# A transformer block on one core: Newton step for the inverse deviation, and set-up work in other places of the program

## The reference

```
x = x + _dwconv(x, pos_w, pos_b)                       # 3 x 3, per channel
x = x + _masa(_layernorm(x, ln1_g, ln1_b), mask_h, mask_w, ...)
y = _layernorm(x, ln2_g, ln2_b)
y = gelu(y @ fc1_w + fc1_b) @ fc2_w + fc2_b            # 64 -> 256 -> 64
return x + y

def _layernorm(x, g, b):
    m = mean(x, -1);  v = mean(square(x - m), -1)
    return (x - m) * rsqrt(v + EPS) * g + b            # EPS = 1e-6
def _masa(x, ...):       # 8 heads of 8 channels
    q, k, v = x @ q_w + q_b, (x @ k_w + k_b) * SCALE, x @ v_w + v_b
    lepe = _dwconv(v, lepe_w, lepe_b)                  # 5 x 5
    attn_w = softmax(q k over each row    + mask_w);  vw  = attn_w v
    attn_h = softmax(q k over each column + mask_h);  out = attn_h vw
    return (out + lepe) @ out_w + out_b
```

## Time and profile before

| | us |
|---|---|
| median of 3 runs (lowest, highest) | 2103.77 (2100.58, 2105.39) |
| profiled execution, its own time | 2106.22 |
| its span in the trace | 2104.4 |
| PE busy / DVE / ACT / POOL | 1852.3 / 1428.2 / 1247.0 / 1173.6 |
| data moved by DMA | 346.82 MB |

### The profile page before, as it was taken

One profiled execution on the slowest core, in us unless ns is written; L12 is line 12 of the kernel. 1 busy time (PEld: TensorE's weight loads), 2 busy tenths in 40 slices (PEclk: granted clock), 3 DMA queues, 4 the chain that ended last, 5 costly groups with the idle time before them and its releaser, 6 DMA issues. The chain is left out here.

```text
span 2104.4 us, 89182 instructions
## 1 busy us (share of the span) xinstructions
PE 1852.3 (88%) x34510; PEld 1548.6 (74%) x34510; DVE 1428.2 (68%) x2270; ACT 1247.0 (59%) x2107; POOL 1173.6 (56%) x1858
## 2 busy tenths in 40 slices
PE   5877624999999999999999999999978995599998
PEld 5877522888887888877887877878768995477776
DVE  3588864777776777766777766767642663688885
ACT  4677734555555555564555555555544766488887
POOL 6477855554555554454555554555534001599997
PEclk8888755999999999999999999999988998799999
DMA  9589566678787787778787787776748994466663
GB/s 141 99 197 223 160 190 148 158 172 180 177 178 167 176 178 177 161 179 186 182 186 175 177 186 172 181 185 161 184 89 148 201 233 142 111 137 137 137 137 82
DMA packets 661152, 346.82 MB, mean 165 GB/s; under 512 B 562462, under 2 KB 613406, under 8 KB 660878
## 3 DMA queue, kind: packets, MB, share of 16 engines
q1 hardware_dynamic: 627782, 298.69, 65.1%
q0 software_dynamic: 31936, 43.83, 7.0%
q10 hardware_dynamic: 1160, 0.13, 0.1%
HBM read 105.42 MB, written 102.76 MB: 99 GB/s over the span
## 5 line engine op out<-in xcount | busy, mean ns | idle before, releaser
L813 ACT ACTIVATE att_prob<-att_st_ps 128x448 f32<-128x448 f32 x896 | 486.9, 544 | 439.0 <-PE att_st_ps L720 438.9
L888 DVE TENSOR_REDUCE att_mm<-att_s_ps 128x8 bf16<-128x448 f32 x896 | 556.2, 621 | 266.9 <-PE att_s_ps L690 263.2
L733 PEld LDWEIGHTS att_pv_ps<-att_vx,att_prob 128*56 128x56 f32 x14336 | 562.0, 132 | 89.2 <-issue 5.6
L733 PE MATMUL att_pv_ps<-att_vx,att_prob 128*56 128x18 f32 x14336 | 514.4, 202 | 5.8 <-ACT att_prob L813 4.3
L582 POOL DMA_DIRECT2D att_mvt<-att_mneg x256 | 136.3, 537 | 555.3 <-ACT att_mneg L802 484.9
L690 PE MATMUL att_s_ps<-att_kx,att_q_unit 120*56 120x448 bf16 x1792 | 347.2, 360 | 9.1 <-DMA att_q_unit<-att_qk_hi 7.4
L715 PE MATMUL att_st_ps<-att_mvt,set_both 122*56 122x448 bf16 x1792 | 345.7, 357 | 9.6 <-DMA att_mvt<-att_mneg 8.3
L720 PE MATMUL att_st_ps<-att_qx,att_k_hi 128*56 128x448 bf16 x1792 | 344.4, 356 | 0.0
L720 PE MATMUL att_st_ps<-att_qx,att_k_lo 128*56 128x448 bf16 x1792 | 342.1, 353 | 0.0
L573 POOL DMA_DIRECT2D att_qx<-att_q_hilo x512 | 245.8, 488 | 2.0 <-issue 1.7
L796 ACT ACTIVATE att_qk_hi<-att_pj,set_bias 128x392 bf16<-128x392 f32 x256 | 150.2, 587 | 124.9 <-PE att_pj L648 124.7
(11 more groups left out here) (209 smaller groups left out, 3196.4 us busy)
## 6 DMA issues: line engine op xcount, KB each, us to landing
att_xt<-xn_chunks SPq DMA_DIRECT2D x128, 196.0 KB, 3.4
att_k_hi<-att_qk_hi SPq DMA_DIRECT2D x128, 196.0 KB, 3.5
att_k_lo<-att_qk_lo SPq DMA_DIRECT2D x128, 196.0 KB, 3.8
att_qx<-att_q_hilo POOLq DMA_DIRECT2D x512, 49.0 KB
pos_x<-in_x_dram SPq DMA_DIRECT2D x128, 105.0 KB
lepe_x<-v_scratch SPq DMA_DIRECT2D x128, 105.0 KB, 4.2
x_scratch<-pos_x SPq DMA_DIRECT2D x128, 98.0 KB
...
```

Source lines behind the costliest of these rows:

```text
L733: ins = pe.matmul(pv_ps[v % 2][64 * h:64 * h + L, at:at + 18], prob[t % 4][:, 4 * h + a, :], vx[v][:, VW * j + 36 * a + 18 * h:VW * j + 36 ...
L813: act.activation(out, src, ACT.Exp).then_inc(exp_done, 1)
L888: dve.tensor_reduce(mm[v % 2][:, NH * j:NH * j + NH], s_ps[j % 2][:, 0:S8].rearrange("p (s k) -> p s k", k=L), AX.X, ALU.max).then_inc(max ...
```

## The change

Four parts.

**Inverse deviation.** POOL's pow is replaced. ACT computes sqrt(v + EPS) (`root`, after the second convolution copy of the image, or behind the high half where the last batch has no copies), DVE takes its reciprocal r0 (`flip`, at the end of DVE's image), and POOL does one Newton step r = r0 (1.5 - 0.5 (v + EPS) r0 r0) in five operations on 128 x 28 (`inverse`). `st` gets a fourth row.

**Masks.** `setup.masks` moves from the identity to behind POOL's sixteen relays of the first batch.

**Start of the attention.** The projections of chunks 2 and 3 on PE (and their high halves on ACT, low halves and values on DVE) go between the first chunk's scores and the second chunk's instead of behind the first maxima; the transposed mask rows are written earlier on DVE; the clear of the second key buffer on ACT is split in two, with the first chunk's negation between; POOL clears its query buffers earlier.

**Feed-forward set-up.** A new class `MlpSetup` holds the parameters' buffers. SP issues their 16 DMAs in the second convolution at n = 7; DVE does the splitting in single steps of that stage at n = 0 and 9 to 14; the identity is shared. In the feed-forward SP starts with four row loads, and its x loads wait only for the memsets of the x buffers.

```diff
+            p = slice(64 * h, 64 * h + 64)
+            sp.dma_start(self.wo_f[p, :], self.wo_d).then_inc(par, 16)
...
+    def settled(self, dve):
+        dve.wait_ge(self.prep, self.steps)
+
+    def clear(self, dve):
+        dve.memset(self.bias_f[:, :, :].rearrange("p n c -> p (n c)"), 0.0).then_inc(self.bias_zero, 1)
+        self.done(dve.memset(self.ones_b[:, :], 1.0))
+        self.done(dve.memset(self.wo2[:, :], 0.0))
...
+    def weights(self, dve, n):
+
+        if n == 0:
+            self.clear(dve)
+        elif n == 9:
+            self.high(dve)
+        elif n == 10:
+            self.low_out(dve)
+        elif n == 11:
+            self.low_first(dve)
...
-                sp.wait_ge(x_clear, 2)
+                sp.wait_ge(x_clear, 3)
                 keys_and_units(i, 1)
...
+                clear(qx[0], q_clear)
                 pool.wait_ge(x_clear, 1)
                 fill_k(pool, i, 0, K_POOL, kx_in_sw)
                 for t in vx:
                     pool.memset(t[:, :], 0.0).then_inc(vx_clear, 1)
-                clear(qx[0], q_clear)
                 pool.wait_ge(q_clear, 1)
                 fill_q(i, 0)
+                clear(qx[1], q_clear)
+                pool.wait_ge(q_clear, 2)
                 pool.wait_ge(mvt_set[0], 1)
                 fill_max(i, 0)
                 pool.wait_ge(ones_set, 1)
                 build_vx(i, 0)
                 build_vx(i, 1)
-                pool.wait_ge(x_clear, 2)
+                pool.wait_ge(x_clear, 3)
                 fill_k(pool, i, 1, K_POOL, kx_in_sw)
                 build_vx(i, 2)
                 pool.wait_ge(vx_done, 12)
-                clear(qx[1], q_clear)
-                pool.wait_ge(q_clear, 2)
                 pool.wait_ge(mvt_set[1], 1)
...
                 for j in range(PAIRS):
                     scores(i, 0, j)
+                    if 2 <= j < 6:
+                        project(i, j // 2 + 1, j % 2)
                 maxima(i, 0)
-                for v in range(2, 4):
-                    for th in range(2):
-                        project(i, v, th)
-                for v in range(2, 4):
-                    project_v(i, v)
                 for j in range(S_EARLY):
                     scores(i, 1, j)
+                    if j in (2, 4):
+                        project_v(i, j // 2 + 1)
...
-                clear(kx[0])
+                clear(kx[0], 0, NH)
                 for v in range(2):
                     for th in range(2):
                         high(i, v, th)
                 unit_rows(q_unit[0])
                 mask_k(0, 0, 4)
-                clear(kx[1])
-                negate(i, 0)
+                clear(kx[1], 0, NH // 2)
                 for v in range(2, 4):
                     for th in range(2):
                         high(i, v, th)
+                negate(i, 0)
+                clear(kx[1], NH // 2, NH)
                 unit_rows(q_unit[1])
...
+                mask_rows_t(0, 0)
                 for v in range(2):
                     for th in range(2):
                         low(i, v, th)
                 for v in range(2):
                     values(i, v)
                 dve.wait_ge(cleared, 8)
+                mask_rows_t(1, 0)
                 for j in range(PAIRS):
                     line_max(i, 0, j)
-                mask_rows_t(0, 0)
+                    if 2 <= j < 6:
+                        low(i, j // 2 + 1, j % 2)
...
-                for v in range(2, 4):
-                    for th in range(2):
-                        low(i, v, th)
-                for v in range(2, 4):
-                    values(i, v)
                 for j in range(S_EARLY):
                     line_max(i, 1, j)
-                mask_rows_t(1, 0)
+                    if j in (2, 4):
+                        values(i, j // 2 + 1)
...
+                    if n == 7:
+                        mlp.parameters(sp)
...
                 identity_on(pool, ident, zeroed, setup.unit)
-                setup.masks(pool)
...
+            def inverse(n):
+
+                u = n % 2
+                var, r, r0 = st[u][:, 1, :], st[u][:, 2, :], st[u][:, 3, :]
+                pool.wait_ge(sd_done, n + 1)
+                pool.tensor_scalar(var, var, EPS, -0.5, ALU.add, ALU.mult).then_inc(eps_done, 1)
+                pool.wait_ge(eps_done, n + 1)
+                pool.wait_ge(flipped, n + 1)
+                pool.tensor_tensor(r, var, r0, ALU.mult).then_inc(newton, 1)
+                pool.wait_ge(newton, 3 * n + 1)
+                pool.tensor_tensor(r, r, r0, ALU.mult).then_inc(newton, 1)
+                pool.wait_ge(newton, 3 * n + 2)
+                pool.tensor_scalar(r, r, 1.5, None, ALU.add).then_inc(newton, 1)
+                pool.wait_ge(newton, 3 * n + 3)
+                pool.tensor_tensor(r, r, r0, ALU.mult).then_inc(rs_done, 1)
...
                 relay(pool, 0, cg, relaid)
             if pos:
+                setup.masks(pool)
                 ahead(0)
...
                         low(pool, n - 1)
-                    pool.wait_ge(var_in, n + 1)
-                    pool.tensor_scalar(st[u][:, 1, :], st[u][:, 1, :], EPS, None, ALU.add).then_inc(eps_done, 1)
-                    pool.wait_ge(eps_done, n + 1)
-                    pool.tensor_tensor(st[u][:, 2, :], st[u][:, 1, :], half[:, :], ALU.pow).then_inc(rs_done, 1)
+                    inverse(n)
                     rezero(n)
                     ahead(n + 1)
...
+            def root(n):
+
+                u = n % 2
+                if n == 0:
+                    act.wait_ge(eps_set, 1)
+                act.wait_ge(var_in, n + 1)
+                if n >= 2:
+                    act.wait_ge(xn_done, n - 1)
+                act.activation(st[u][:, 2, :], st[u][:, 1, :], ACT.Sqrt, bias=eps[:, 0:1]).then_inc(sd_done, 1)
...
                     for cg in range(4):
                         conv_copy(b + 1, 4 * q + cg)
+                        if pos and cg == 1:
+                            root(n)
                         if not pos and q < 2 and cg % 2 == 0:
                             high(n + q + cg // 2)
                 if pos:
+                    if b + 1 == NBATCH:
+                        root(n)
                     ahead(n + 1)
...
+            def flip(n):
+                dve.wait_ge(sd_done, n + 1)
+                if n >= 2:
+                    dve.wait_ge(rs_done, n - 1)
+                dve.reciprocal(st[n % 2][:, 3, :], st[n % 2][:, 2, :]).then_inc(flipped, 1)
...
                         col_copy(n - 2, range(2, G))
+                    flip(n)
...
-            sp.wait_ge(bias_zero, 1)
-            for k in range(3):
-                sp.dma_start(bias_f[32 * k:32 * k + 1, 0, :], bo_d.unsqueeze(0)).then_inc(par, 16)
-            sp.dma_start(b2[:, :], bf2_d.partition_broadcast(128)).then_inc(par, 16)
-            sp.wait_ge(gaps, 1)
-            for v in range(NV - 1):
+            for v in range(4):
+                sp.dma_start(rt[v][:, :], rt_d[v]).then_inc(rt_in[v], 16)
+            sp.wait_ge(cleared, 4)
+            for v in range(4):
+                for r in range(2):
+                    sp.dma_start(x1[v][64 * r:64 * r + L, :, :], x1_v[v, r]).then_inc(x1_in[v], 16)
+            for v in range(4, NV - 1):
                 load(0, v)
...
             for t in x1[0:4]:
-                done(dve.memset(t[32:64, :, :].rearrange("p j c -> p (j c)"), 0.0))
+                dve.memset(t[32:64, :, :].rearrange("p j c -> p (j c)"), 0.0).then_inc(cleared, 1)
             for t in (*o_ps[0:2], *y_ps):
-                done(dve.memset(t[:, :], 0.0))
-            settled()
-            dve.sem_inc(gaps, 1)
-            dve.wait_ge(par, 16 * 16)
...
-            for k in range(3):
-                done(dve.tensor_copy(bias_3[32 * k:32 * k + 32, :, :], bias_p[k][32 * k:32 * k + 32, :, :]))
+                dve.memset(t[:, :], 0.0).then_inc(cleared, 1)
+            dve.wait_ge(cleared, 8)
+            dve.sem_inc(ready, 1)
             dve.wait_ge(pre_pe, 1)
-            done(dve.tensor_tensor(b1[:, :], h_ps[0][:, 0:2], b1_in[:, :], ALU.add))
-            dve.wait_ge(unit, 1)
-            done(dve.tensor_copy(ident_b[:, :], ident[:, :]))
-            settled()
-            dve.sem_inc(ready, 1)
+            dve.tensor_tensor(b1[:, :], h_ps[0][:, 0:2], b1_in[:, :], ALU.add).then_inc(biased, 1)
             front(0, 0)
             front(0, 1)
```

176 lines of the change are left out of this document (98 added, 78 removed).

## The result

The changed kernel took 2079.09 us, the median of 4 runs (2071.65 to 2082.95), against 2103.81 before: a ratio of 0.988, 95% interval 0.9849 to 0.9911. That is 24.7 us less, where 28.8 were forecast. Its profiled execution, the slowest of the four, took 2082.95, with a span of 2081.2 against 2104.4. The span is thus 23.2 us shorter. Where they lie is told by the starts of the stages, SP's first issue in each (DVE's first memset for the feed-forward).

| stage | before | after | difference | forecast |
|---|---|---|---|---|
| positional convolution, layernorm | 318.4 | 297.3 | -21.1 | -19.8 |
| attention | 1247.0 | 1245.0 | -2.0 | 0 |
| second convolution | 221.5 | 230.9 | **+9.4** | +0.2 |
| feed-forward | 317.6 | 308.1 | -9.5 | -10.3 |

The account below looks back on a forecast made before the run. It took a loop between engines through POOL's pow to bound the positional convolution; 17.8 (Newton) + 2.0 (masks) + 0 (attention) + 10.1 (feed-forward set-up) = 29.9 us less, stated as 2075, range 2065 to 2090.

Parts of the forecast that it names:

- the lock moves: Positional convolution: POOL's relays now slow DVE's centring instead of its scale, 1.9 us per image, giving 2080; chance 0.25.
- the set-up does not do what it says: Feed-forward start: x's loads wait for other stores, only 5 of the 10 us come, giving 2080; chance 0.05.
- own mechanism: Whole kernel: the forecast's gains come as described, without the rivals' losses, giving 2067 to 2079; chance 0.47.
- The loop through pow is the bound, and DVE is next: Positional convolution: an engine loop of 12.73 us sets the tail's pace; without pow, DVE's own work of 11.8 does.
- Stretches: Positional convolution, four consecutive windows: gains of 2.3, 5.7, 3.4 and 6.4 us, the second ending in a DMA wait.
- Table loads cost nothing: ACT, convolution and attention's start: separate loads for Sqrt and Exp fall where ACT waits for PE; 0, at worst 2.6.
- Masks: Positional convolution's start: four mask DMAs issued later let the first relay come 2.1 us earlier; gain 2.0 (0 to 2.1).
- Attention: Attention's start: earlier projections only lengthen PE's wait for the DMA of the unit's queries; 0, bounds -3 and +3.
- Feed-forward: Feed-forward's start: sixteen parameter DMAs leave its head, so the first residual sum comes earlier; gain 10.3 (8.5 to 11).
- The second convolution: Second (lepe) convolution: takes on 16 SP issues and some ten DVE operations of the feed-forward set-up; cost 0.2 us.
- The bounds: Whole kernel: the bounds of the parts added in full are given as 17 and 35 us of gain.
- Newton: Positional convolution: root, reciprocal and five POOL operations replace pow, 2.4 us for 5.1 per image; stage gain 17.8.

Follow-up runs that it names:

- e2: Changed kernel with the inverse deviation by pow on POOL as before, all else as changed: positional stage 318.5 us, 18.9 us more than e1 in the medians.
- g1: Changed kernel with both convolutions' tiles aligned by 32-byte buffers, plus DVE's reciprocal moved between an image's last two column copies: ratio 0.9853 to the kernel before.
- e1: Changed kernel once more, unaltered: second convolution 229.8 us, ratio 0.9886 to the kernel before.
- e3: Changed kernel with the feed-forward's parameters issued and split at the head of the feed-forward again: 2094.91 us, second convolution 230.7.

## Why the prediction was right, and where it was not

The prediction gave 2075 (2065 to 2090), the measured time is 2079.09, and its sum of 29.9 us stands against 24.7. The number alone would fit the rivals "the lock moves" and "the set-up does not do what it says" (2080 each) better than the own mechanism (2067 to 2079); only the stages tell them apart. By its steps:

- **The loop through pow is the bound, and DVE is next.** Right: with pow put back the stage is 20.0 us longer (e2), where 17.8 were forecast. The tail's loop is 11.56 for 11.8, and the reciprocal, which was bounded by 0.2 and 0.5 and taken at 0.3, takes 0.32.
- **Stretches.** 3.4, 5.6, 3.9 and 7.1 for 2.3, 5.7, 3.4 and 6.4. The second is best supported: its end was forecast from SP's chain and the DMA share, and the relay there did change its waiting from POOL to DMA.
- **Table loads cost nothing.** Right. The drain of 1.38 us that the Trainium skill ("ScalarE: Activation LUTs", What ACT_TABLE_LOAD costs) gives did not show behind the first either: the root began 0.01 us later. Nor does it lie ahead of a load: the second, at 329.81, began 0.01 us after ACT's operation before it had ended.
- **The lock moves.** Right as a mechanism. As a rival's price it was too dear: with 1.9 us on each image it gave 0.5 and 0 us for the first and third stretches, which gained 3.4 and 3.9, and the excess over both operations grew from 12.6 to 15.6 us only. The rule of the Trainium skill ("SBUF — State Buffer", Who interferes with whom) agrees with the row at 132.70 in that the two shut each other out: the centring took 1.92 us more beside relays of 1.96. That the first to issue wins, which the prediction took from there and saw in the earlier trace rows, these rows do not show: by their recorded starts both the scale and the centring had begun first, by 0.07 and 0.09 us, and it was they that took longer. The row of g1 at 144.68 agrees with it: there the centring was first by 0.25 us and POOL waited.
- **Masks.** The relay's 2.0 was right (2.15), but the forecast let it through to the end. The first mean came 1.2 earlier, because PE's granted clock rose no earlier (37.4 us, 37.6 before) and the earlier convolutions ran on the lower level for longer; the forecast had no term for that.
- **Attention.** 0 was right; the bounds of 3 held. That PE would wait longer was wrong in its place: it waited for the negated maxima, not for the second unit's queries. The first exponentials mostly came later, since the negation on ACT, which they need, now comes 6 to 8 us later, and later chunks made up for it.
- **Feed-forward.** 9.5 for 10.3.
- **The second convolution, the step that failed.** The forecast costed the operations and DMAs that the change adds there, at 0.2 us, and they do cost about nothing: with and without them (e1 and e3) the stage takes 229.8 and 230.7. It put at nothing the buffers that come to stand ahead of the convolution's. Their place took 9.4 us between the two profiles, 7 to 8 by the timed runs. The rival "set-up does not do what it says", 5 of 10 lost, has the right sign and the wrong place: the feed-forward got its gain.
- **The bounds.** The prediction says that those of its parts add up to 17 and 35. They don't: its own bounds, 8.5 to 23.5 for Newton, 0 to 2.1 for the masks, -3 to 3 for the attention and some 8.5 to 11 for the feed-forward, make 14 and 39. The range of 2065 to 2090 happens to be as wide as that.

So one term was off by 9 us and the point by only 4. That is luck in part: other terms erred the other way, Newton by 2.2, and the attention by 2.0 in the one profile, which is within its spread. Without them the result would still have been inside the range, which had been made wide for other losses than the one that came.
